# Attention heads on two groups of 64 TensorE rows, scores given from opposite groups, and a third PSUM bank for the row scores

## The chip, the cores and the metric

The kernel runs on one core of a Trainium2 chip. The metric is the device time of one execution in microseconds (us). TensorE is written PE (its weight loads PEld), VectorE DVE, ScalarE ACT, GpSimd POOL, and SyncE SP.

## What is computed

A macaron block on x of 16 items x 256 tokens x 128 features: half a mixture-of-experts layer (8 experts, the best 2 for each token), attention, and half the same mixture again.

```python
x = x + 0.5 * ffn(layernorm(x), ...)
x = x + attn(layernorm(x), ...)
x = x + 0.5 * ffn(layernorm(x), ...)

# attn: 16 heads of 4 features, of the left 64 features of x, softmax over the keys
q = (left @ Wq.T).reshape(N, S, H, Dh)      # N=16, S=256, H=16, Dh=4
k, v = ...                                   # likewise
att = softmax(einsum('nqhd,nkhd->nqkh', q, k) / scale, axis=2)
out = einsum('nqkh,nkhd->nqhd', att, v).reshape(N, S, 64) @ Wo.T + bo
```

## The kernel before

The first mixture, the attention and the second mixture follow each other. In the attention each engine runs the same loop by hand-written order: `run_steps` goes over steps s = 0 to 18, and each step has 16 units k (`UR` = 16). In step s the row scores of item s are made, the column scores, exponentials and most of the values of item s - 2, the last values and the output of item s - 3, and the projection of item s + 2.

Head operands. `qa` and `ka` hold, per item (four buffers in turn), q and k split into bf16 pieces: 24 rows (`KP`), and 2 more rows (`KM` = 26) that bring in the row maxima against rows of ones. They are `[128, 16 heads, 256]`, and only 26 of the 128 rows hold anything; a matmul runs over all 128. SP fills them through DRAM: `sp_pieces` writes the pieces, `sp_operands` reads them back with six DMAs, `sp_max` adds the maxima with two.

Scores. Unit k of a step has two matmuls of `pe_rows` (line 896, two heads of one half of the queries, 256 keys each) into one PSUM bank, from which DVE takes the maxima (`dve_max`, line 1179), and two of `pe_cols` (line 880, head k) into bank 3 or 4, from which ACT takes exponentials (`act_exp`, line 1000). `pe_rows` has banks 0 and 1 in turn (`SA`) and so waits for the maxima of two units earlier (`attn_max_done`); `pe_cols` waits for the exponential of two units earlier (`attn_exp_done`).

PE's order in a unit is: the two `pe_cols` matmuls, then whatever `AT` puts into this unit (transposes of the normed x, of the maxima, of the outputs; the output product `pe_out`, line 958; the projection `pe_project`, lines 931 and 933), then the two `pe_rows` matmuls, then the values (`pe_values`, line 908, fp32, sixteen records for four heads, each head on its own 32 columns of the array) in units 1, 5, 9 and 13. All of it is fp32 but the scores and the maxima.

Banks 5 (values), 6 and 7 (`MISC_A`, `MISC_B`) serve the rest; `misc_free` makes a user of bank 6 or 7 wait for the one before it. From step 5 the routing of the second mixture is made inside these steps, in two halves: a step with odd s has statistics, norm, transpose (unit 6) and logits (unit 11, lines 275 and 278), the one after it the choice, the positions and, for some groups, the lists. The routing uses bank 2 for all of that, and nobody else does. DVE's `dve_residual` (line 1210) adds the output product to x in unit 12, `dve_otok` (lines 1197 and 1201) divides the outputs in units 6 and 10.

## Time and profile before

| what | us |
|---|---|
| median of three runs (range) | 837.45 (835.38 to 838.81) |
| the profiled execution | 832.24 |
| its span on the core | 830.5 |
| PE busy, share of the span | 616.5 (74%) |
| DVE busy | 431.9 (52%) |
| ACT busy | 343.6 (41%) |
| POOL busy | 378.1 (46%) |
| first row scores (start) | 283.4 |
| first and last item's maxima closed | 300.8 and 602.6 |

The page gives busy time over the whole span; what a change in the attention is worth is read from the stretch between 283 and 640 us alone. PE's matmuls are pipelined and the ends shown are modelled: two matmuls of a group that start 0.11 us apart are each shown 0.27 us long, so PE's use is read from starts, and the moment at which a result can be used from the start of the engine that waits for it.

### The profile page before, as it was taken

The page shows a single profiled execution, that of the slowest core. Times are in us where ns is not written, and L with a number is a line of the kernel's source. Part 1 is how long each engine was busy: PE and PEld are TensorE (multiplying, and loading weights), DVE is VectorE, ACT ScalarE, POOL GpSimd, SP SyncE. Part 2 cuts the span into 40 slices and gives each one's busy share as a digit, 9 for nine tenths or more (in the row PEclk, how much of TensorE's full clock was granted, in tenths as well). Part 3 has the DMA queues.
Part 4 walks back from the last instruction along what each step waited for, and adds up shares of the span by engine and source line. Part 5 has one row for each costly group of instructions (what it writes and reads, how often), then busy time and mean ns, then how long its engine had stood idle before and what let it go on. Part 6 is the DMA issues. An engine that isn't in the chain of part 4 may idle for free. (4 is left out here: it accounts for less than half of the span.)

```text
span 830.5 us, 14400 instructions
## 1 busy us (share of the span) xinstructions
PE 616.5 (74%) x4460; PEld 449.2 (54%) x4460; DVE 431.9 (52%) x1607; ACT 343.6 (41%) x806; POOL 378.1 (46%) x421
## 2 busy tenths in 40 slices
PE   4318877999971288898888788888866778999850
PEld 3216766889960125555444555554533567887740
DVE  7633333232331387678777777757743343344425
ACT  2003333455530015665555555645554333454430
POOL 4775342000017886444666665432231465555452
PEclk9998798999995558999999999979998788999995
DMA  9453344655511121111212111101000435544428
GB/s 298 131 169 124 124 135 131 198 163 176 173 45 39 56 70 47 43 48 47 64 50 64 51 61 47 54 34 45 15 19 18 141 120 166 174 155 145 136 64 301
DMA packets 65026, 86.01 MB, mean 104 GB/s; under 512 B 11096, under 2 KB 46648, under 8 KB 64152
## 3 DMA queue, kind: packets, MB, share of 16 engines
q1 hardware_dynamic: 52184, 63.29, 23.6%
q0 software_dynamic: 8640, 17.97, 7.0%
q10 hardware_dynamic: 4128, 3.83, 1.4%
q8 instruction: 37, 0.61, 0.3%
q14 instruction: 37, 0.30, 0.1%
HBM read 31.85 MB, written 30.56 MB: 75 GB/s over the span
## 5 line engine op out<-in xcount | busy, mean ns | idle before, releaser
L1179 DVE TENSOR_REDUCE attn_nm<-ps 128x2 f32<-128x512 f32 x256 | 168.7, 685 | 71.7 <-PE ps L896 65.6
L671 DVE SCALAR_TENSOR_TENSOR experts_act<-ps,route_cols,experts_silu 128x256 f32<-128x256 f32 x170 | 80.0, 483 | 201.9 <-ACT experts_silu L635 137.9
L1000 ACT ACTIVATE attn_pt<-ps 128x512 f32<-128x512 f32 x256 | 145.6, 594 | 93.8 <-PE ps L880 76.4
L603 PE MATMUL ps<-experts_xT,experts_w 128*128 128x256 f32 x680 | 178.9, 409 | 0.1
L379 POOL DMA_INDIRECT x_rows<-route_xn,route_rows x128 | 124.8, 975 | 83.6 <-DVE route_rows L363 48.9
L896 PE MATMUL ps<-attn_ka,attn_qa 128*128 128x256 bf16 x512 | 107.9, 298 | 47.6 <-DVE attn_nm L1179 36.4
L603 PEld LDWEIGHTS ps<-experts_xT,experts_w 128*128 128x128 f32 x680 | 131.4, 204 | 17.6 <-issue 0.5
L614 PE MATMUL ps<-w_table,experts_act 128*128 x680 | 106.8, 295 | 28.9 <-ACT experts_y_tokens L652 14.0
L635 ACT ACTIVATE experts_silu<-ps,route_cols 128x256 f32<-128x256 f32 x170 | 78.4, 476 | 108.8 <-PE ps L603 83.8
L614 PEld LDWEIGHTS ps<-w_table,experts_act 128*128 128x128 f32 x680 | 93.9, 199 | 35.4 <-issue 33.8
L880 PE MATMUL ps<-attn_qa,attn_ka 128*128 128x256 bf16 x512 | 101.5, 282 | 13.2 <-ACT attn_pt L1000 8.2
L707 POOL DMA_INDIRECT y_tokens<-experts_y_tokens,experts_to x78 | 74.7, 957 | 68.2 <-ACT experts_y_tokens L652 50.6
L896 PEld LDWEIGHTS ps<-attn_ka,attn_qa 128*128 128x128 bf16 x512 | 39.6, 101 | 87.8 <-DVE attn_nm L1179 56.4
L908 PE MATMUL ps<-attn_pt,attn_va 128*32 128x256 f32 x1024 | 73.8, 409 | 1.0 <-ACT attn_pt L1000 1.0
L880 PEld LDWEIGHTS ps<-attn_qa,attn_ka 128*128 128x128 bf16 x512 | 41.2, 100 | 56.8 <-issue 34.1
L1077 POOL DMA_INDIRECT attn_yg<-y_rows,route_y_at x64 | 62.2, 973 | 15.8 <-issue 14.7
L1104 POOL MEMSET attn_va<- 128x1024 f32 x5 | 4.8, 963 | 115.0 <-DMA y_rows<-experts_y_tokens 115.0
L592 PE MATMUL ps<-ident,experts_x 128*128 128x128 f32 x170 | 34.6, 288 | 14.3 <-issue 7.8
L908 PEld LDWEIGHTS ps<-attn_pt,attn_va 128*32 128x32 f32 x1024 | 27.8, 113 | 27.5 <-issue 11.0
L1101 POOL TENSOR_TENSOR attn_kqp<-attn_rem,attn_kqp 128x256 bf16<-128x256 f32 x16 | 10.7, 667 | 68.7 <-ACT attn_kqp L1041 68.7
L641 ACT ACTIVATE experts_xT<-ps 128x256 f32<-128x256 f32 x85 | 32.6, 383 | 21.0 <-PE ps L592 13.1
L592 PEld LDWEIGHTS ps<-ident,experts_x 128*128 128x128 f32 x170 | 24.3, 150 | 26.9 <-issue 12.0
(165 smaller groups left out, 733.3 us busy)
## 6 DMA issues: line engine op xcount, KB each, us to landing
experts_w<-w_table SPq DMA_DIRECT2D x85, 256.0 KB
experts_x<-x_rows SPq DMA_DIRECT2D x85, 132.0 KB
y_rows<-experts_y_tokens SPq DMA_DIRECT2D x46, 128.0 KB, 1.7
x_rows<-no_rows SPq DMA_DIRECT2D x24, 132.0 KB
kq_pieces<-attn_kqp SPq DMA_DIRECT2D x16, 192.0 KB
x_rows<-route_xn,route_rows POOLq DMA_INDIRECT x128
second_y<-y_tokens SPq DMA_DIRECT2D x8, 256.0 KB, 6.9
second_y<-y_tokens ACTq DMA_DIRECT2D x8, 256.0 KB, 7.3
```

The source lines that it names most:

```text
L379: nc.gpsimd.indirect_dma_start(out=x_rows[REGION_OF[group_part(g)] % 2][:, :], out_offset=to, in_=xn[:, g % RX, t, :], in_offset=None).the ...
L603: mm = pe.matmul(ps[:, q % 2 * 2 + k, w * SLOTS:(w + 1) * SLOTS], m["w"][:, q % WR, at + k * P:at + (k + 1) * P], m["xT"][:, q % 2], start ...
L614: pe.matmul(o, m["act"][:, q % 2, k, i * P:(i + 1) * P], of_expert(w2_table, e, k * P, P), start=(k == 0), stop=False)
L635: nc.scalar.activation(m["silu"][:, q % 2, k], ps[:, q % 2 * 2 + k, 0:SLOTS], ACT.Silu, bias=route["col"](part, at, k)).then_inc(silu_done, 1)
L671: nc.vector.scalar_tensor_tensor(out=m["act"][:, q % 2, k], in0=ps[:, q % 2 * 2 + k, SLOTS:2 * SLOTS], scalar=route["col"](part, at, CH + ...
L707: nc.gpsimd.indirect_dma_start(out=y_tokens[:, :], out_offset=to, in_=m["y_tokens"][:, q % YR, i, :], in_offset=None).then_inc(y_sent[q % ...
L880: mm = pe.matmul(ps[:, SBK[h % 2], kc * S:(kc + 1) * S], ka[sl][:, h, kc * P:(kc + 1) * P], qa[sl][:, h, :], start=True, stop=True)
L896: mm = pe.matmul(ps[:, SA[k], j * S:(j + 1) * S], qa[sl][:, h, qc * P:(qc + 1) * P], ka[sl][:, h, :], start=True, stop=True)
L908: mm = pe.matmul(ps[32 * j:32 * j + 32, O, (g % 2) * S:(g % 2 + 1) * S], va[b % VR][:, kc, NJ * g + j, :], pt[:, g % 2, j, kc * S:(kc + 1) ...
L1000: nc.scalar.activation(pt[:, g % 2, j, :], ps[:, SBK[h % 2], :], ACT.Exp, scale=SCALE).then_inc(exp_done, 1)
L1077: nc.gpsimd.indirect_dma_start(out=yg[:, b % YG, t, r, :], out_offset=None, in_=y_rows[:, :], in_offset=route["y_offset"](2 * b + t, r)).t ...
L1179: nc.vector.tensor_reduce(nm[:, qc, 2 * pair:2 * pair + 2], ps[:, SA[k], :].rearrange("p (j t) -> p j t", t=S), AX.X, ALU.max, negate=True ...
```

## The change

- `qa` and `ka` become `[128, 8, 256]`: heads 0 to 7 lie on rows 0 to 63, heads 8 to 15 on rows 64 to 127, 26 rows used of each 64. The score matmuls name their group of 64 rows (`tile_position`).
- `pe_cols` and `pe_rows` are given one matmul at a time and in turn. Row scores begin with the heads of the upper group (`row_unit`), column scores with those of the lower, so that neighbours in PE's order lie on opposite groups.
- The row scores have three banks (0, 1, 2), and wait for the maxima of three units earlier. Bank 2 was the routing's; the routing's transposes and positions go to bank 6, logits and part sums (`cols`) to bank 7, and they wait there for the user before them, as others now wait for them.
- The other work of a unit comes after the unit's scores. `AT` changes: turned 6, xT 9, otok1 5, oTs 8, out 10, logits 12, positions 4, cols 14 of the second step; ACT's and DVE's units follow (residual 11).
- SP's six operand DMAs become twelve of half the size, its two for the maxima become four, the one of ones two. The zeroing of `qa` and `ka` is halved.

```diff
-    SA = (0, 1) * 8
+    SA = (0, 1, 2)
+    HH = NH // 2
...
-    AT = dict(xT=8, otok0=11, project=13, mT=2, otok1=6, oTs=10, out=12, values3=1, values0=5)
+    AT = dict(turned=6, xT=9, otok0=11, project=13, mT=2, otok1=5, oTs=8, out=10, logits=12, values3=1, values0=5,
+              positions=UR + 4, cols=UR + 14)
+    USES = {MISC_A: ("positions", "turned", "xT", "otok0", "project"), MISC_B: ("mT", "otok1", "oTs", "out", "logits", "cols")}
...
+    def half(t, r):
+        return t[r * P // 2:(r + 1) * P // 2]
+
+    def row_unit(k):
+        r = 1 - k // HH
+        pair, qc = divmod(k % HH, 2)
+        return r * HH // 2 + pair, qc
...
-    def pe_cols(pe, b, sl, h):
+    def pe_cols(pe, b, sl, h, kc):
...
+        r, at = divmod(h, HH)
+        mm = pe.matmul(ps[:, SBK[h % 2], kc * S:(kc + 1) * S], half(ka[sl], r)[:, at, kc * P:(kc + 1) * P],
+                       half(qa[sl], r)[:, at, :], start=True, stop=True, tile_position=(r * P // 2, 0))
+        if kc:
+            mm.then_inc(cols_ready, 1)
...
-        if not first(n, ago):
-            wait(pe, max_done, n - ago + 1)
-        for j in range(2):
...
+            if not first(n, len(SA)):
+                wait(pe, max_done, n - len(SA) + 1)
+        r, at = divmod(2 * pair + j, HH)
+        mm = pe.matmul(ps[:, SA[n % len(SA)], j * S:(j + 1) * S], half(qa[sl], r)[:, at, qc * P:(qc + 1) * P],
+                       half(ka[sl], r)[:, at, :], start=True, stop=True, tile_position=(r * P // 2, 0))
...
         for k in range(UR):
-            if valid(s - 2):
-                pe_cols(pe, s - 2, (sl - 2) % 4, k)
+            for i in range(2):
+                if valid(s - 2):
+                    pe_cols(pe, s - 2, (sl - 2) % 4, k, i)
+                if valid(s):
+                    pe_rows(pe, s, sl, k, i)
...
-            if valid(s):
-                pe_rows(pe, s, sl, k)
...
-            if u == 11:
+            if u == AT["logits"]:
+                misc_free(pe, s, MISC_B, "logits")
                 route["pe_logits"](pe, GROUPS + g)
...
+        for r in range(2):
+            heads = slice(r * HH * S, (r + 1) * HH * S)
...
+            for n in (3, 2, 1):
+                sp.dma_start(kv[at:at + n * DH, :], kq[0:n, 0]).then_inc(ops_in, 16)
...
         for i in range(KM - KP):
-            sp.dma_start(qa[sl][KP + i:KP + i + 1], mT[NH * i:NH * i + NH, :]).then_inc(m_in, 16)
+            for r in range(2):
+                at = NH * i + HH * r
+                sp.dma_start(half(qa[sl], r)[KP + i:KP + i + 1], mT[at:at + HH, :]).then_inc(m_in, 16)
...
-                qa.append(sb(f"qa{i}", [P, NH, S], BF16)[:])
-                ka.append(sb(f"ka{i}", [P, NH, S], BF16)[:])
+                qa.append(sb(f"qa{i}", [P, HH, S], BF16)[:])
+                ka.append(sb(f"ka{i}", [P, HH, S], BF16)[:])
```

**PE, the end of units 11 to 13 in a step with a routing's first half.** Before (L896 row scores, L880 column scores, L275 and L278 logits, L958 output product; a row's waits in brackets):

```order
L896 MATMUL ps<-attn_ka,attn_qa 128x256 [waits attn_max_done]
L896 MATMUL ps<-attn_ka,attn_qa 128x256
L275 MATMUL ps<-gate_b_sb,ident 128x32 [waits route_xT_done]
L278 MATMUL ps<-gate_w_sb,route_xT 128x8 x4
L880 MATMUL ps<-attn_qa,attn_ka 128x256 [waits attn_exp_done]
L880 MATMUL ps<-attn_qa,attn_ka 128x256
L958 MATMUL ps<-wo,attn_oTs 128x128 [waits attn_oTs_copied]
L958 MATMUL ps<-wo,attn_oTs 128x128
L896 MATMUL ps<-attn_ka,attn_qa 128x256 [waits attn_max_done]
L896 MATMUL ps<-attn_ka,attn_qa 128x256
L880 MATMUL ps<-attn_qa,attn_ka 128x256 [waits attn_exp_done]
L880 MATMUL ps<-attn_qa,attn_ka 128x256
```

After (L927 row scores, L911 column scores, L285 and L288 logits, L963 the projection):

```order
L911 MATMUL ps<-attn_qa,attn_ka 128x256 [waits attn_exp_done]
L927 MATMUL ps<-attn_ka,attn_qa 128x256 [waits attn_max_done]
L911 MATMUL ps<-attn_qa,attn_ka 128x256
L927 MATMUL ps<-attn_ka,attn_qa 128x256
L285 MATMUL ps<-gate_b_sb,ident 128x32 [waits route_xT_done,attn_x_updated]
L288 MATMUL ps<-gate_w_sb,route_xT 128x8 x4
L911 MATMUL ps<-attn_qa,attn_ka 128x256 [waits attn_exp_done]
L927 MATMUL ps<-attn_ka,attn_qa 128x256 [waits attn_max_done]
L911 MATMUL ps<-attn_qa,attn_ka 128x256
L927 MATMUL ps<-attn_ka,attn_qa 128x256
L963 MATMUL ps<-attn_xT,wqk 128x256 [waits attn_norm_done,attn_xT_done]
```

The scores now alternate one by one; the logits have moved behind the scores of unit 12 and wait for `attn_x_updated`, the end of DVE's residual; the output product, which stood between the scores of unit 12, has moved to unit 10.

**DVE, from unit 10 of such a step on.** Before (L1197 and L1201 divide the outputs, L1179 is a maximum, L1210 the residual):

```order
L1197 RECIPROCAL attn_rsum<-ps 128x16 [waits attn_norm_done,attn_otok_ready]
L1201 TENSOR_TENSOR attn_otok<-ps,attn_rsum 128x2x32 [waits attn_oTs_ready,attn_recip_done]
L1179 TENSOR_REDUCE attn_nm<-ps 128x2 [waits attn_rows_ready] x2
L1210 TENSOR_TENSOR x_tokens<-x_tokens,ps 128x256 [waits attn_bias_added,attn_y_ready]
L1179 TENSOR_REDUCE attn_nm<-ps 128x2 [waits attn_rows_ready]
```

After (L1234 and L1238, L1216, L1247):

```order
L1234 RECIPROCAL attn_rsum<-ps 128x16 [waits attn_norm_done,attn_otok_ready]
L1238 TENSOR_TENSOR attn_otok<-ps,attn_rsum 128x2x32 [waits attn_oTs_ready,attn_recip_done]
L1216 TENSOR_REDUCE attn_nm<-ps 128x2 [waits attn_rows_ready]
L1247 TENSOR_TENSOR x_tokens<-x_tokens,ps 128x256 [waits attn_bias_added,attn_y_ready]
L1216 TENSOR_REDUCE attn_nm<-ps 128x2 [waits attn_rows_ready] x2
```

The residual stands one maximum earlier than it did.

**SP, one step in the middle of the attention.** Before, all operand DMAs of a step and the two of the maxima:

```order
L1271 DMA attn_ka<-kq_pieces 12x1x4096
L1271 DMA attn_ka<-kq_pieces 8x1x4096
L1271 DMA attn_ka<-kq_pieces 4x4096
L1275 DMA attn_qa<-kq_pieces 12x1x4096
L1275 DMA attn_qa<-kq_pieces 8x1x4096
L1279 DMA attn_qa<-kq_pieces 6x4096
L1284 DMA attn_qa<-attn_mT 1x16x256 x2
```

After, the last DMA of the first group of heads, the six of the second, and the four of the maxima:

```order
L1318 DMA attn_qa<-kq_pieces 6x2048
L1311 DMA attn_ka<-kq_pieces 12x1x2048
L1311 DMA attn_ka<-kq_pieces 8x1x2048
L1311 DMA attn_ka<-kq_pieces 4x2048
L1315 DMA attn_qa<-kq_pieces 12x1x2048
L1315 DMA attn_qa<-kq_pieces 8x1x2048
L1318 DMA attn_qa<-kq_pieces 6x2048
L1325 DMA attn_qa<-attn_mT 1x8x256 x4
```

The maxima's DMAs stand behind twelve others now, where they stood behind six.

## Rows read from the trace of the kernel before

**Rows 1.** Page, costliest group: xcount | busy us, mean ns | idle before, releaser

```profile
L1179 DVE TENSOR_REDUCE attn_nm<-ps 128x2 f32<-128x512 f32 x256 | 168.7, 685 | 71.7 <-PE ps L896 65.6
```

**Rows 2.** Busy time by attention step: stretch, length, busy us of each engine, clock, DMA

```profile
300.80:316.30 15.50, 12.41 (x46) 4.69 (x46) 13.01 (x27) 2.43 (x6) 13.53 (x16) 0.50 0.20 59
...
412.70:434.70 22.00, 17.83 (x169) 10.85 (x167) 16.82 (x62) 11.67 (x27) 13.46 (x15) 1.00 0.18 54
434.70:454.30 19.60, 16.52 (x160) 9.44 (x159) 14.78 (x44) 11.36 (x25) 12.40 (x14) 1.00 0.20 60
...
476.10:496.60 20.50, 17.96 (x159) 10.29 (x157) 14.71 (x45) 11.31 (x25) 12.42 (x15) 0.92 0.19 58
...
537.40:564.80 27.40, 23.62 (x168) 14.69 (x166) 16.96 (x61) 12.10 (x27) 7.04 (x8) 0.75 0.10 34
...
sum 301.80, PE 256.15 PEld 151.02 DVE 224.40 ACT 164.15 POOL 152.14; mean PE 17.08 PEld 10.07 DVE 14.96 ACT 10.94 POOL 10.14
```

**Rows 3.** Waits from 300 to 600: who waited, on whom, total us, times, longest

```profile
PE ps L896 <- DVE attn_nm L1179: 32.6, 57, 1.7
```

**Rows 4.** Timeline 444 to 453: start, us, engine, line, operation, tiles [idle before]

```profile
445.25 1.07 PE L908 MATMUL ps<-attn_pt,attn_va 128*32 128x256 f32 x16
...
447.57 0.38 PE L896 MATMUL ps<-attn_ka,attn_qa 128*128 128x256 bf16 x2
...
447.79 0.38 PE L880 MATMUL ps<-attn_qa,attn_ka 128*128 128x256 bf16 x2
...
448.10 0.71 PE L958 MATMUL ps<-wo,attn_oTs 64*128 64x128 f32 x4
...
448.74 0.39 PE L896 MATMUL ps<-attn_ka,attn_qa 128*128 128x256 bf16 x2
...
450.46 0.69 DVE L1179 TENSOR_REDUCE attn_nm<-ps 128x2 f32<-128x512 f32 x1 [1.16 <-PE ps L896]
```

**Rows 5.** Timeline at 716, eight full-array fp32 matmuls of 256 columns

```profile
716.05 1.95 PE L603 MATMUL ps<-experts_xT,experts_w 128*128 128x256 f32 x8
```

**Rows 6.** Timeline 384 to 394, a step with a routing's first half

```profile
384.92 0.60 PE L943 MATMUL ps<-ident,attn_oT 128*128 128x128 f32 x4
...
385.72 1.04 PE L278 MATMUL ps<-gate_w_sb,route_xT 128*128 128x8 f32 x8
385.85 0.22 DVE L1201 TENSOR_TENSOR attn_otok<-ps,attn_rsum 128x64 f32<-128x64 f32 x1
...
388.60 0.41 DVE L1210 TENSOR_TENSOR x_tokens<-x_tokens,ps 128x256 f32<-128x256 f32 x1
```

**Rows 7.** Five-microsecond windows (PEclk 1.00 is 2.4 GHz, 0.50 is 1.2 GHz)

```profile
475.00:480.00 5.00, 3.29 (x37) 1.63 (x37) 4.54 (x16) 2.85 (x7) 2.60 (x3) 1.00 0.28 74
480.00:485.00 5.00, 4.45 (x31) 2.40 (x32) 3.46 (x14) 2.44 (x6) 3.61 (x5) 0.69 0.28 91
555.00:560.00 5.00, 5.00 (x20) 3.53 (x20) 1.02 (x2) 1.19 (x2) 0.00 (x0) 0.50 0.00 0
```

**Rows 8.** SP's queue in two steps, and the matmul that comes next

```profile
307.92 1.22 SPq L1284 DMA_DIRECT2D attn_qa<-attn_mT  x2
...
315.24 0.64 PE L880 MATMUL ps<-attn_qa,attn_ka 128*128 128x256 bf16 x2
...
436.84 1.93 SPq L1271 DMA_DIRECT2D attn_ka<-kq_pieces  x3
...
440.69 1.17 SPq L1284 DMA_DIRECT2D attn_qa<-attn_mT  x2
...
453.15 0.38 PE L880 MATMUL ps<-attn_qa,attn_ka 128*128 128x256 bf16 x2
```

**Rows 9.** Timeline, start of attention

```profile
283.03 1.80 POOL L1110 MEMSET attn_ka<- 128x2048 uint32 x1
...
283.44 1.03 PE L896 MATMUL ps<-attn_ka,attn_qa 128*128 128x256 bf16 x4 [7.34 <-DMA attn_qa<-kq_pieces]
...
286.61 2.07 DVE L1179 TENSOR_REDUCE attn_nm<-ps 128x2 f32<-128x512 f32 x3
```

More of the change, by code:

```diff
@@ L207, in bank, with through @@
         return BANK[g]
+    def through(name, g):
+        part = group_part(g)
+        if name == "positions" and ends_part(g):
+            return [(prod_done, g + 1), (list_step, listing(part) + 1)]
+        return [dict(turned=(xT_done, g + 1), logits=(index_done, g + 1), positions=(prod_done, g + 1),
+                     cols=(cols_done, part + 1))[name]]
     def closed_parts(part):
```

153 lines of the change are left out of this document (78 added, 75 removed).

## The prediction

> **What bounds the kernel now.** I read first where the attention spends DVE's time. The costliest group of the page is the maxima of the row scores, 256 of 685 ns, with 71.7 us of idle time before them, 65.6 of it ended by PE [rows 1]. The stretches by step are the second view [rows 2]; each reaches from the row that closes one item's maxima (line 1187) to the next such row. The fifteen from 300.8 to 602.6 us take 301.8 us, 20.1 each, and over them (last row) DVE is busy 224.4 of 301.8 us, so it stands idle 77.4, 5.2 a step. The 22.0 us step from 412.7 has a routing's first half and 16.8 us of DVE work, the 19.6 us step from 434.7 the second half and 14.8. No engine is full, then: PE and DVE hold each other up. The waits show both directions. Besides DVE's wait for PE, PE's row scores wait 32.6 us for the maxima, 57 times, the longest 1.7 us [rows 3]: with two banks PE can be only two units ahead.
>
> The timeline shows where which wait ends last [rows 4]. In the last third of a step PE never rests: a score pair takes 0.22 us (starts 447.57 and 447.79), then the output product, then scores again, and the maximum of unit 12 starts only at 450.46, 1.16 us of DVE's time lost. Its scores started at 448.74 and are shown over at 449.13, so the result reached DVE 1.3 us late. In the first third, where DVE has the routing's or the item's statistics to make, DVE is the busy one and PE waits (4.54 and 3.29 of 5 us from 475 to 480) [rows 7]. A gain in PE's score time therefore counts in about a third of a step, and a longer lead of PE over DVE counts at its beginning.
>
> **The change part by part.** Steps that have both kinds of scores are s = 2 to 15, fourteen; six of them (5, 7, ... 15) carry a routing's first half.
>
> *Scores from opposite groups.* A unit costs PE 4 matmuls, two pairs of 0.22 us, 0.44 [rows 4]. If neighbours run side by side it is 0.22, if not 0.44: the saving is 0 to 0.22. The trace of before has no two row groups, but it has four column groups: sixteen fp32 records of 256 columns take 1.07 us [rows 4], eight on the full array 1.95 [rows 5], so 0.067 against 0.24 each, 3.6 times as fast with four groups. I take 0.21 a unit, that nearest row. It counts in five units (10 to 14) of a step: 1.05 us, ends 0 and 1.1.
>
> *The third bank.* PE may be one maximum further ahead, 0.69 us [rows 1], when its long stretch begins; it also covers that much of a late result. I take 0.69 once a step, ends 0 and 1.4 (twice a step, since the values of unit 5 or 9 begin a smaller such stretch).
>
> Together 1.74 us in each of the eight steps without logits: 13.9. In steps 0 and 1, with row scores alone and no neighbours on the other group, only the bank: 1.4.
>
> *Logits behind the residual.* This is a new wait: PE's logits in unit 12 wait for `attn_x_updated`, and behind them in PE's queue stand the scores of unit 13, the projection and the values, for which DVE and ACT wait. From the start of the outputs' transposes to the end of DVE's division is 1.15 us (384.92 to 386.07), then DVE makes one maximum, 0.69, and the residual, 0.41: 2.25 us [rows 1, 6]. PE has in this time the transposes (shown 0.60) and the scores of unit 12 (0.22): it waits about 1.4 us, and then the logits' 1.04 us [rows 6] follow, before which nothing of unit 13 can be given. That eats the 1.74. I leave these six steps 0.5 us each for what they gain in unit 5 and 9: 3.0, ends -1 and 1.7 a step. The other new waits in banks 6 and 7 are for releases at least two units old, and I cost them at nothing; DVE's and ACT's work of those units is their cover.
>
> *More changes of the array's shape.* Leaving the scores for the output product costs 0.31 us from start to start where 0.22 is usual (447.79 to 448.10) [rows 4], so about 0.1 for a change. Before, a step changed at the values (four times there and back), at the output product and the projection: 12 changes. After, output and projection have the scores' shape, and the transposes of mT, otok1, xT, oTs and otok0 have not: 16, and 2 to 4 more with routing. In the last third it is 4 instead of 6, in the middle third 8 instead of 4, half of which I put on the path: 0.2 us x 14 = 2.8 lost. The Trainium skill (TensorEngine Tiling (Array Packing), Key Properties) says that changing the tiling mode, not just the tile, drains the TensorE; by a full drain, of the length that the last matmul of a pair is shown to have, the loss would be some 7 us rather than 2.8. The row at 448.10 shows 0.1, and I stay with it.
>
> *DMAs.* SP issues six operand DMAs in 3.85 us (436.84 to 440.69) and the maxima's two after them [rows 8]. Twelve take 7.7 if an issue of half the size costs the same. In a later step the maxima's DMAs then start at 444.5 instead of 440.7, and the columns that need them start at 453.15 [rows 8]: 8.6 us are left, less what the step gets shorter, and that hides them. In the first steps it is not: the maxima of item 0 are issued from 307.92 and their columns start at 315.24 [rows 8]; 3.85 us later, and four (2.4 us) instead of two, they are all issued at 314.2, and PE waits for whatever their landing takes over 1 us. No row has that landing alone; I take a wait of 2, ends 0 and 4. At the start the first scores come at 283.44, ended by the operands' DMAs; DVE's first maximum at 286.61, held by POOL, which zeroes ka in 1.80 us (and qa before it) [rows 9]. Halving both gives DVE 1.8 us, twice the issues takes 3.85 from PE: between -1.8 and +3.3, I take 1. Together 3.0 lost.
>
> *The clock.* In the steps from 412.7 and 434.7 the granted clock is 1.00, the 2.4 GHz level [rows 2]. At 475 to 480 PE is busy 3.29 of 5 us, and in the window after that it falls for a part (0.69 on the mean) [rows 7]. Shorter scores leave PE less busy in the first third, so I expect such falls in most steps. The price of a short one: the step from 476.1 (0.92) is 20.5 us, that from 434.7 (1.00) with the same work 19.6 [rows 2]: up to 0.9, 0.4 as a mean over some eight: 3.0 lost.
>
> Sum: 13.9 + 1.4 + 3.0 - 2.8 - 3.0 - 3.0 = 9.5 us gained. The second mixture begins when the attention ends and shifts with it. Against the profiled execution, 832.24, that is 822.7; the median of the runs shown is 837.45, 5.2 above it, and the same 9.5 us make **828.0**.
>
> **The rivals.** (1) *DVE becomes the only bound.* Concurrency, the bank and the cover of late results work everywhere, and DVE's idle time falls to what the first step shows, 15.50 - 13.01 = 2.5 us [rows 2]. 14 steps with 5.3 instead of 2.5: 39 us, less 3 for DMAs: 801. For it: PE's waits for DVE show that PE could run ahead. Against it: logits, clock. (2) *No concurrency*: weights and matmuls of the two groups go one after the other. Left are the bank, 0.69 x 8 + 1.4 = 6.9, half of the six steps' 3.0, and the losses by shape and DMA (5.8), no fall of the clock: about 835. (3) *The clock stays low*, slower: once the low-activity first third takes it down, the half clock lasts, as it does from 555 to 560 us at least (0.50 throughout, the 1.2 GHz level), in a step of 27.4 us instead of 22.0 [rows 2, 7]: 5.4 us a spell. Four such spells more are 21.6, against 12.5 gained (the sum without its 3.0 for short falls): 846. It decides from three spells on. (4) *The change doesn't do what it says because SP sets the pace*: the half-size DMAs are issued and landed too slowly, and the maxima's rows come after the columns want them in every step; then a step stays near 20 us, 837.
>
> **How the numbers follow.** Forecast 0.43, (1) 0.18, (2) 0.14, (3) 0.16, (4) 0.09. The range takes in the forecast's ends, the larger part of (1) and of (3): 803 to 845. What a measurement can tell from no change is 0.5%, 4.2 us. Faster: 0.40 + 0.18 + 0.05 = 0.63; slower: 0.15 + 0.03 of (4) and (2) = 0.18; the rest, 0.19, within.
>
> **What would show it.** Concurrency: four score matmuls of a unit within about 0.22 us of starts, and L911 and L927 starting nearly together; 0.44 says rival 2. The bank: PE's wait for the maxima well below 32.6 us and DVE's wait for PE below 65.6. Logits: a PE wait of 1 to 2 us before L285 in six steps, ended by DVE's L1247. DMAs: a PE wait for the maxima's DMA at the first column scores, and 12 issues in 7 to 8 us; more such waits in later steps say rival 4. Clock: several windows of the attention below 1.00 where they were 1.00. I am wrong in size if steps without logits are not 1 to 2 us shorter than 19.6, and in sign if the half clock lasts over 7 us at a time.

## The result, and the profile of the changed kernel

The changed kernel takes 852.0 us, the median of 5 runs (842.6 to 853.4), the kernel before beside it 835.8. The ratio is 1.0175, 95% interval 1.012 to 1.023: slower by 15 us (16 by the medians) where I had forecast 9.5 faster, and above the upper end of my range, 845. The profiled execution took 842.55 us (span 840.7), the shortest of the five; against the 832.24 (span 830.5) of the profiled execution of before its span is 10.2 us longer. The granted clock is 0.851 in the mean; before it was 0.893.

The page first. The idle time before the maxima fell, as forecast, from 71.7 to 56.2 us [rows 1], but that before ACT's exponentials is 104.4 us, 93.8 before, and the scores, half as many rows high, are no shorter on the mean (310 and 319 ns, before 282 and 298). Columns: xcount | busy us, mean ns | idle before, releaser.

```profile
L1216 DVE TENSOR_REDUCE attn_nm<-ps 128x2 f32<-128x512 f32 x256 | 165.9, 684 | 56.2 <-PE ps L927 43.4
L1037 ACT ACTIVATE attn_pt<-ps 128x512 f32<-128x512 f32 x256 | 145.8, 595 | 104.4 <-PE ps L911 93.7
...
L911 PE MATMUL ps<-attn_qa,attn_ka 64*128 64x256 bf16 x512 | 107.7, 310 | 40.1 <-ACT attn_pt L1037 30.8
...
L927 PE MATMUL ps<-attn_ka,attn_qa 64*128 64x256 bf16 x512 | 109.8, 319 | 18.3 <-DMA attn_qa<-kq_pieces 11.1
```

The stretches by step stand in the same form as in [rows 2], now from one closing of the maxima (line 1224) to the next.

```profile
300.10:314.40 14.30, 10.54 (x42) 4.91 (x42) 12.19 (x27) 2.47 (x6) 11.56 (x15) 0.50 0.22 66
...
348.70:365.20 16.50, 12.86 (x152) 6.44 (x152) 13.46 (x33) 11.43 (x26) 8.52 (x11) 1.00 0.20 56
...
388.80:411.00 22.20, 16.61 (x145) 7.14 (x137) 14.89 (x45) 10.69 (x22) 11.14 (x13) 0.73 0.16 47
411.00:434.30 23.30, 19.58 (x188) 9.14 (x187) 17.38 (x61) 13.27 (x29) 14.71 (x17) 0.83 0.19 56
434.30:453.00 18.70, 12.56 (x137) 6.37 (x136) 14.81 (x44) 10.22 (x23) 11.07 (x13) 1.00 0.19 57
...
536.50:563.40 26.90, 20.21 (x182) 11.02 (x186) 17.23 (x61) 13.13 (x29) 7.34 (x9) 0.79 0.13 40
...
sum 305.40, PE 238.93 PEld 115.24 DVE 226.72 ACT 164.89 POOL 149.68; mean PE 15.93 PEld 7.68 DVE 15.11 ACT 10.99 POOL 9.98
```

The fifteen steps take 305.4 us instead of 301.8 [rows 2], and DVE stands idle in 78.7 of them, as good as before (77.4): what the maxima gained was lost elsewhere. The steps split into three kinds. The four without routing (s = 1 to 4, of which the first and the last are shown) take 65.1 us, before 71.6: 6.5 gained. The six that give logits (s = 5, 7, ... 15; shown from 411.0 and 536.5) take 144.1, before 133.9: 10.2 lost. The five between them (shown from 388.8 and 434.3) take 96.2, before 96.3: nothing. The column of the granted clock (the third from the end) points at one reason: most steps are no longer at 1.00, and the step from 388.8 at 0.73 takes 22.2 us, that from 434.3 at 1.00 takes 18.7. It isn't the whole reason, since 411.0 and 536.5 are logits steps too. If f is the granted clock of a stretch of t us, 2(1 - f)t of it ran at the lower level, 1.2 GHz: 78 us of the eleven steps from 365.2 to 605.5, in 16 falls, and 21 before, in 4. Thirteen of the 16 spells are short, some 3 us; the longest two last 13.7 us. The end of the attention, in which only column scores are left, shows it once more. First the changed kernel, then the kernel before:

```profile
605.50:647.70 42.20, 34.07 (x257) 15.29 (x255) 13.65 (x80) 20.77 (x42) 8.96 (x9) 0.71 0.05 14
```

```profile
602.60:639.80 37.20, 26.82 (x261) 14.41 (x257) 13.98 (x81) 20.85 (x42) 8.95 (x9) 0.94 0.05 16
```

Sum of the span: -0.7 to the end of the first step, -6.5, +10.2, -0.1, +5.0 in this last stretch and +2.3 in the second mixture make 10.2.

The waits, 300.1 to 605.5 us: who waited, on whom, total us, times, longest.

```profile
ACT attn_pt L1037 <- PE ps L911: 83.6, 70, 5.2
...
DVE attn_nm L1216 <- PE ps L927: 42.9, 38, 2.9
...
PE ps L285 <- DVE x_tokens L1247: 7.1, 5, 1.9
...
PE ps L927 <- DVE attn_nm L1216: 4.2, 10, 0.9
...
PE ps L911 <- DMA attn_qa<-attn_mT: 2.0, 1, 2.0
```

PE's wait for the maxima is 4.2 us; it was 32.6 [rows 3]. The logits wait 7.1 us for the residual, 1.4 a time. Here is one, in a step with a routing's first half (start, us, engine, line, operation, tiles, idle before):

```profile
508.70 0.41 DVE L1247 TENSOR_TENSOR x_tokens<-x_tokens,ps 128x256 f32<-128x256 f32 x1
...
509.02 0.68 DVE L1216 TENSOR_REDUCE attn_nm<-ps 128x2 f32<-128x512 f32 x1
...
509.16 0.41 PE L285 MATMUL ps<-gate_b_sb,ident 128*128 128x32 f32 x2 [1.41 <-DVE x_tokens L1247]
...
509.41 1.04 PE L288 MATMUL ps<-gate_w_sb,route_xT 128*128 128x8 f32 x8
...
510.38 0.28 PE L911 MATMUL ps<-attn_qa,attn_ka 64*128 64x256 bf16 x1
...
512.09 0.60 ACT L1037 ACTIVATE attn_pt<-ps 128x512 f32<-128x512 f32 x1 [3.03 <-PE ps L911]
512.13 0.69 DVE L1216 TENSOR_REDUCE attn_nm<-ps 128x2 f32<-128x512 f32 x1 [2.42 <-PE ps L927]
```

PE stands from its last scores until the residual, 1.41 us, then gives the gate's bias and the logits, and only at 510.38 the scores of unit 13. DVE had one maximum in hand (509.02) and ACT nothing. The scores are shown over at 510.77, but both engines start on them only at 512.09 and 512.13: ACT has lost 3.03 us, DVE 2.42. So there is a late result on top of the wait. A purer case stands in the step that starts at 434.3:

```profile
449.17 0.27 PE L927 MATMUL ps<-attn_ka,attn_qa 64*128 64x256 bf16 x1
...
449.42 0.96 POOL L389 DMA_INDIRECT x_rows<-route_xn,route_rows  x1 [0.30 <-issue]
451.69 0.60 ACT L1037 ACTIVATE attn_pt<-ps 128x512 f32<-128x512 f32 x1 [2.47 <-remote]
451.73 1.29 DVE L1216 TENSOR_REDUCE attn_nm<-ps 128x2 f32<-128x512 f32 x2 [2.05 <-remote]
...
452.43 0.27 PE L911 MATMUL ps<-attn_qa,attn_ka 64*128 64x256 bf16 x1 [2.99 <-ACT attn_pt L1037]
```

The last score starts at 449.17 and is shown 0.27 us long; ACT and DVE start 2.5 us after its start, 2.3 after its shown end, having stood idle for 2.47 and 2.05, and PE, which needs the banks that they free, for 2.99. POOL issues indirect DMAs in that time. In the trace of before, in the same routing, a result came 1.3 us after the shown end [rows 4]. What follows on the clock, over the time in which PE had nothing (columns as in the stretches by step):

```profile
449.70:452.90 3.20, 0.47 (x4) 0.22 (x4) 1.18 (x2) 1.21 (x3) 0.90 (x2) 1.00 0.12 40
453.10:456.30 3.20, 3.17 (x26) 0.99 (x26) 2.98 (x14) 1.66 (x3) 2.60 (x4) 0.50 0.30 82
```

PE is busy 0.47 of 3.2 us, still at 1.00, and behind that the clock is 0.50, the level of 1.2 GHz, while PE is busy 3.17 of 3.2. All 16 falls of the eleven steps come behind a stretch with such gaps, most of them smaller: before the one at 408.6, for example, PE is busy 1.83 of 3.3 us.

```profile
405.20:408.50 3.30, 1.83 (x24) 1.43 (x26) 2.35 (x6) 2.23 (x5) 0.00 (x0) 1.00 0.06 20
```

### The profile page after: what moved, and what is told of

Same layout as the page of the kernel before. It is cut to its first block and busy times, and to the rows that moved or that the text cites. A ratio compares the mean times of both kernels' runs of the same rounds, so it can differ in the third digit from the quotient of the medians.

```text
span 840.7 us, 14542 instructions
## 1 busy us (share of the span) xinstructions
PE 602.3 (72%) x4460; PEld 413.0 (49%) x4460; DVE 431.5 (51%) x1607; ACT 344.2 (41%) x806; POOL 372.7 (44%) x421
## 5 line engine op out<-in xcount | busy, mean ns | idle before, releaser
L1216 DVE TENSOR_REDUCE attn_nm<-ps 128x2 f32<-128x512 f32 x256 | 165.9, 684 | 56.2 <-PE ps L927 43.4
L1037 ACT ACTIVATE attn_pt<-ps 128x512 f32<-128x512 f32 x256 | 145.8, 595 | 104.4 <-PE ps L911 93.7
L911 PE MATMUL ps<-attn_qa,attn_ka 64*128 64x256 bf16 x512 | 107.7, 310 | 40.1 <-ACT attn_pt L1037 30.8
L927 PE MATMUL ps<-attn_ka,attn_qa 64*128 64x256 bf16 x512 | 109.8, 319 | 18.3 <-DMA attn_qa<-kq_pieces 11.1
L911 PEld LDWEIGHTS ps<-attn_qa,attn_ka 64*128 64x128 bf16 x512 | 36.5, 99 | 111.0 <-issue 56.4
L940 PE MATMUL ps<-attn_pt,attn_va 128*32 128x256 f32 x1024 | 89.2, 478 | 0.7 <-ACT attn_pt L1037 0.7
L927 PEld LDWEIGHTS ps<-attn_ka,attn_qa 64*128 64x128 bf16 x512 | 36.9, 103 | 32.3 <-DVE attn_nm L1216 14.5
L940 PEld LDWEIGHTS ps<-attn_pt,attn_va 128*32 128x32 f32 x1024 | 31.0, 127 | 32.6 <-issue 21.6
L602 PE MATMUL ps<-ident,experts_x 128*128 128x128 f32 x170 | 34.4, 287 | 13.7 <-DMA experts_x<-x_rows 7.1
L651 ACT ACTIVATE experts_xT<-ps 128x256 f32<-128x256 f32 x85 | 32.6, 383 | 24.7 <-PE ps L602 14.7
L251 POOL TENSOR_TENSOR route_rstd<-route_vare,neg_half 128x4 f32<-128x4 f32 x16 | 16.7, 1046 | 48.7 <-DVE route_vare L246 48.1
```

The lines of the kernel that those rows point to most:

```text
L911: mm = pe.matmul(ps[:, SBK[h % 2], kc * S:(kc + 1) * S], half(ka[sl], r)[:, at, kc * P:(kc + 1) * P], half(qa[sl], r)[:, at, :], start=Tru ...
L927: mm = pe.matmul(ps[:, SA[n % len(SA)], j * S:(j + 1) * S], half(qa[sl], r)[:, at, qc * P:(qc + 1) * P], half(ka[sl], r)[:, at, :], start= ...
L940: mm = pe.matmul(ps[32 * j:32 * j + 32, O, (g % 2) * S:(g % 2 + 1) * S], va[b % VR][:, kc, NJ * g + j, :], pt[:, g % 2, j, kc * S:(kc + 1) ...
L1037: nc.scalar.activation(pt[:, g % 2, j, :], ps[:, SBK[h % 2], :], ACT.Exp, scale=SCALE).then_inc(exp_done, 1)
L1216: nc.vector.tensor_reduce(nm[:, qc, 2 * pair:2 * pair + 2], ps[:, SA[(UR * b + k) % len(SA)], :].rearrange("p (j t) -> p j t", t=S), AX.X, ...
```

## The experiments

The kernel before was timed again in each comparison, and it is not equally quick on every chip: 835.8 us beside the changed kernel above, 819.0, 739.5, 821.0, 820.2 and 831.5 in the five comparisons below. So every result is a ratio to the kernel before in its own comparison, with its 95% interval.

Three theories stood at the start. **A**: the shorter scores let PE's clock fall, and that eats more than the overlap of the two groups gives. **B**: the logits' wait and the shared banks. **C**: the doubled number of SP's DMAs.

### First comparison (the kernel before: 819.0 us)

**e1: the same 64 rows for both scores of a unit.**

```
-        r = 1 - k // HH
+        r = k // HH
```

> One line differs from the changed kernel: the row scores go through the heads in the other order, so that the row scores of a unit stand on the same 64 rows as its column scores and the four matmuls of a unit can only follow each other (0.44 us instead of 0.22). Nothing else moves. Theory A (the shorter scores leave PE so little to do that its clock falls, and the half clock costs more than the overlap gives): mean granted clock back from 0.85 to about 0.89, no more half-clock stretches than before the change, time 828 to 838, 15 to 20 us below the changed kernel's 852. Theory B (the logits' wait behind the residual and the shared banks 6 and 7): the waits stay, 850 to 858. Theory C (twelve and four DMAs on SP instead of six and two): also unchanged, 850 to 858.

Measured: 875.2 us, 1.059 (1.048 to 1.070), granted clock 0.79 to 0.81. All three theories are wrong about this one. Neighbours now can't overlap, and they don't:

```profile
350.78 0.28 PE L911 MATMUL ps<-attn_qa,attn_ka 64*128 64x256 bf16 x1
350.90 0.27 PE L927 MATMUL ps<-attn_ka,attn_qa 64*128 64x256 bf16 x1
```

A unit of four takes 0.44 us; in the changed kernel two start together, and the next two 0.12 us later, 0.23 a unit:

```profile
446.07 0.28 PE L911 MATMUL ps<-attn_qa,attn_ka 64*128 64x256 bf16 x1
446.07 0.28 PE L927 MATMUL ps<-attn_ka,attn_qa 64*128 64x256 bf16 x1
...
446.19 0.27 PE L911 MATMUL ps<-attn_qa,attn_ka 64*128 64x256 bf16 x1
...
446.30 0.27 PE L911 MATMUL ps<-attn_qa,attn_ka 64*128 64x256 bf16 x1
```

So the overlap is real and worth having, about 4% against 1.019 of the changed kernel in a comparison of like speed (below). But longer scores did not bring the clock back, as A had it: PE is busier (677 us instead of 602) and the clock lower. The low spells are fewer and much longer. One begins at 589.6, behind 3.2 us in which PE was busy 0.64, and lasts 44 us, with PE shown busy throughout:

```profile
589.60:633.80 44.20, 44.20 (x261) 23.27 (x262) 25.38 (x79) 19.02 (x36) 9.50 (x10) 0.50 0.09 28
```

**e2: one group of rows, the rest of the change kept** (operands, DMAs and score order of before; three banks; routing in banks 6 and 7).

```
-        r, at = divmod(h, HH)
-        mm = pe.matmul(ps[:, SBK[h % 2], kc * S:(kc + 1) * S], half(ka[sl], r)[:, at, kc * P:(kc + 1) * P],
-                       half(qa[sl], r)[:, at, :], start=True, stop=True, tile_position=(r * P // 2, 0))
+        mm = pe.matmul(ps[:, SBK[h % 2], kc * S:(kc + 1) * S], ka[sl][:, h, kc * P:(kc + 1) * P],
+                       qa[sl][:, h, :], start=True, stop=True)
...
```

> The changed kernel with its first part undone: the heads on one group of rows with six operand DMAs and the scores in the order of before (columns first, rows behind the unit's other work); three banks and the routing in banks 6 and 7 stay. A: no more clock falls, the third bank's gain is left, 825 to 835. B: the loss stays, 845 to 855. C: also 825 to 838, so that this run alone doesn't tell A from C.

Measured: 818.1 us, 0.994 (0.990 to 0.999). The expected 825 to 835 went with a kernel before of 835.8, and as a ratio 0.994 lies among them. The loss is gone, and the gain is small. The run takes away the two groups together with their DMAs and their order of scores; f2 and z1 below show that, with full rows, neither of these costs anything.

**e3: the two groups alone**, on the kernel before (two banks, routing in bank 2, all units as before).

```
-    SA = (0, 1) * 8
+    SA = (0, 1)
+    HH = NH // 2
...
+            for i in range(2):
+                if valid(s - 2):
+                    pe_cols(pe, s - 2, (sl - 2) % 4, k, i)
+                if valid(s):
+                    pe_rows(pe, s, sl, k, i)
...
```

> The kernel before with the first part of the change alone: two groups of rows, scores given in turn, twelve and four DMAs; two banks for the row scores, the routing in bank 2 and all other work in its units of before. A: clock falls as in the changed kernel, 845 to 860. B: the logits wait for nothing, and the overlap gains what I forecast, 820 to 830. C: as A, 845 to 855.

Measured: 851.3 us, 1.036 (1.027 to 1.044), clock 0.83. The groups lose 3.6% without any logits' wait and with two banks, so B is not the whole cause. A or C is left for this part.

**e4: every score matmul given twice.**

```
+        for _ in range(2):
             mm = pe.matmul(ps[:, SBK[h % 2], ...
...
```

> The changed kernel with every score matmul of the attention given twice in a row (the second writes the same result again), so that PE does twice the score work, as long as before the change, on both groups of rows. A: the clock rises to 0.90 or more and the time falls by 10 to 20 us although PE has more to do, 832 to 842. B and C: nothing to gain, 0.44 us more in each unit of the stretches where PE sets the pace, 855 to 870.

Measured: 870.9 us, 1.061 (1.056 to 1.067), clock 0.87 to 0.88. The clock does rise from 0.85, and it doesn't pay: PE's added work costs more. That is about the upper end of what B and C had given.

e1 and e4 suggested a new form of A: not how long PE is busy, but on how many of its rows. In e1 PE is busy longer than in the kernel before (677 us against 616.5), and the clock falls further.

### Second comparison (739.5 us)

**f1: the kernel before with its scores on 64 rows.** The other rows hold zeros, so that the result is the same.

```
-                           qa[sl][:, h, qc * P:(qc + 1) * P], ka[sl][:, h, :], start=True, stop=True)
+                           qa[sl][0:P // 2, h, qc * P:(qc + 1) * P], ka[sl][0:P // 2, h, :], start=True, stop=True)
...
```

> The kernel before with one difference: the score matmuls take the 64 rows of PE that hold the pieces, instead of all 128 of which the upper 70 are zeros. Nothing is given side by side, no DMA, order or bank differs, and the matmuls are as long. Theory A in its new form (PE's clock follows how much of the array works, and scores on 64 rows halve that): mean granted clock 0.80 to 0.83 instead of 0.90, time 850 to 865 where the kernel before has 819. Theory D (the loss of the two groups comes from side-by-side work itself or from the changes between the groups): no difference, 817 to 824. Theory C (DMAs): no difference either.

Measured: 843.0 us, 1.143 (1.137 to 1.149), clock 0.76 to 0.79 where the kernel before has 0.92. This is the largest effect of the study, more than twice what was expected, from an edit that moves and removes nothing. (Rows with something in them are 26 of 128, so 102 hold zeros, not 70.) Its step at 439.0, without logits:

```profile
439.00:460.10 21.10, 20.70 (x159) 10.60 (x158) 14.85 (x44) 11.72 (x25) 12.07 (x14) 0.76 0.18 56
```

and the same step of f2 (next), which has full rows and is as quick as the kernel before:

```profile
398.30:416.20 17.90, 15.97 (x158) 9.68 (x157) 14.73 (x44) 11.33 (x25) 12.30 (x14) 1.00 0.22 66
```

The matmuls are the same 158 or 159, DVE's work is 14.7 to 14.9 us in both, and the clock is 0.76 instead of 1.00. The 20.70 us of PE's busy time don't say that the clock fell under full work, since matmuls at the lower level take twice as long and so fill the step. What happened is seen when the stretch is cut where the level changes: before the fall at 415.1, then at the lower level, then behind the rise at 449.2.

```profile
411.60:415.00 3.40, 1.92 (x18) 1.00 (x22) 3.32 (x11) 1.98 (x5) 2.13 (x3) 1.00 0.23 61
415.20:449.20 34.00, 34.00 (x188) 17.91 (x180) 18.28 (x64) 13.40 (x27) 14.80 (x18) 0.50 0.15 47
449.30:460.10 10.80, 10.40 (x95) 6.08 (x94) 7.93 (x16) 6.95 (x16) 6.46 (x8) 1.00 0.09 27
```

The fall comes behind gaps, as in the changed kernel. But then PE is busy 34.00 of 34.00 us, on half of its rows, and the level stays at 1.2 GHz. This repeats every two steps, with the same 34 us. So what the halved rows take away is above all the return of the clock: f2 falls once in its fifteen steps, for a short spell, and the longest low spell that begins in these steps of the kernel before is 10 us. Falls without a gap exist too, two of f1's seven. Behind this stretch the clock is 0.50 again:

```profile
377.70:380.90 3.20, 3.20 (x27) 2.60 (x26) 1.77 (x4) 1.04 (x2) 0.00 (x0) 1.00 0.00 0
```

Both such stretches have the logits in them, eight matmuls of only 8 columns shown 1.04 us long, so that "busy" is not "full". More changes of shape between scores and transposes are no rival for f1's loss: at the full clock its pairs of scores start 0.22 us apart and lose 0.1 at a change, as before [rows 4]. The Trainium skill (TensorE: Matmul & The Clock Gate, HAM oscillation) ties falls of the clock to gaps in which PE has no matmuls. The late result at 449 of the changed kernel agrees with it, and so do five of f1's seven falls; two do not.

**f2: SP's DMAs cut as in the changed kernel**, twelve and four, on tiles of before.

```
+        for half in range(2):
+            heads = slice(half * HH * S, (half + 1) * HH * S)
...
```

> The kernel before with SP's DMAs cut as in the changed kernel: the operands in twelve instead of six, each with half of the heads, the maxima in four instead of two. Tiles, matmuls, order and banks are those of before. A: 819 to 823, only the first steps lose. C (twelve and four DMAs are what costs): 840 or more. My prediction's own term was 3.0 us.

Measured: 738.0 us, 0.998 (0.996 to 1.000). C falls; my term of 3.0 us for DMAs was a loss that isn't there.

**e6: the logits one unit later.**

```
-    AT = dict(turned=6, xT=9, otok0=11, project=13, mT=2, otok1=5, oTs=8, out=10, logits=12, values3=1, values0=5,
+    AT = dict(turned=6, xT=9, otok0=11, project=13, mT=2, otok1=5, oTs=8, out=10, logits=13, values3=1, values0=5,
...
-            if u == 14:
+            if u == 15:
                 route["dve_top"](dve, GROUPS + g)
```

> The changed kernel with the logits one unit later (13 instead of 12) and the top values behind unit 15 instead of 14. If PE's wait for the residual (7.1 us in five logits steps of the changed kernel's trace) is on the path, 845 or a little less, 5 to 7 below the changed kernel; if the clock sets the time of these steps, no difference, 850 to 854.

Measured: 726.5 us, 0.981 (0.978 to 0.984), clock 0.89 to 0.90. Faster than the kernel before, on a quick chip; whether by the edit or by the chip this comparison doesn't tell, and it was repeated below.

**f5: one matmul on all 128 rows more in each unit**, overwritten by the row scores.

```
+        if j == 0:
+            pe.matmul(ps[:, SA[n % len(SA)], 0:S], qa[sl][:, 0, 0:P], ka[sl][:, 0, :], start=True, stop=True)
```

> The changed kernel with one matmul more in each of the 256 units, on all 128 rows of PE, 256 columns, whose result the row scores overwrite: 0.11 us each, 28 us of PE's time in all, of which the stretches where PE sets the pace would pay about 10. A: the array works more, the mean granted clock rises from 0.84 to 0.87 or more, and the time is no longer than the changed kernel's, 840 to 852. If array work has nothing to do with the clock: clock 0.84, time 860 or more.

Measured: 784.3 us (775.3 to 790.3), 1.063 (1.055 to 1.071), profiled clock 0.90. The expectation had named times of the slower chip. Against e6 in the same comparison it is 58 us more, most of which the logits' unit can't be; the clock is no help at that price.

### Third comparison (821.0 us)

**g0: the changed kernel itself.**

> The changed kernel itself, on the chip on which the next three run, since the kernel before took 835.8, 819.0 and 739.5 us in three comparisons and the loss may depend on what makes the difference. Where the kernel before has 0.90 or less of mean granted clock, 1.01 to 1.02 of its time; where it is as quick as 740 us, 0.98 to 1.00, because the logits one unit later gave 0.981 there.

Measured: 836.8 us, 1.019 (1.011 to 1.027), clock 0.847. The result repeats on a second chip.

**g1: e6 again, beside it.**

> The changed kernel with the logits in unit 13 and the top values behind unit 15, again, now beside the changed kernel. If the wait for the residual is on the path: 5 to 7 us less than the changed kernel in the same comparison. If the clock sets the time of these steps: within 2 us of it.

Measured: 819.3 us, 0.998 (0.994 to 1.002). That is 17.5 us less than the changed kernel, 2.1%: the whole loss, and more than either side of the expectation had. Its six logits steps take 121.7 us in its trace, against 144.7 in that of g0, and the five between them give 6.5 of it back (103.7 and 97.2). One logits step of each, g0 first; the second has slightly more of the full clock and is 2.9 us shorter:

```profile
450.30:473.00 22.70, 18.97 (x187) 9.27 (x183) 17.17 (x61) 12.67 (x28) 14.45 (x16) 0.87 0.19 57
```

```profile
441.70:461.50 19.80, 16.46 (x168) 8.60 (x170) 15.68 (x46) 12.14 (x27) 13.66 (x16) 0.91 0.20 60
```

**g2: e2 again, one group of rows.**

> The third bank and the moved routing without the two groups of rows, again (the run of this edit before had 0.994 of the kernel before). Against the changed kernel in the same comparison this is the price of the two groups: 10 to 20 us below the changed kernel where the kernel before has a granted clock of 0.90 or less, and within 10 us of it or above it where it has 0.92.

Measured: 815.8 us, 0.994 (0.991 to 0.998), 21 us below the changed kernel. Two of its steps, and the sum of its fifteen:

```profile
428.70:447.00 18.30, 14.60 (x137) 8.89 (x137) 14.76 (x43) 10.32 (x23) 11.10 (x13) 1.00 0.19 57
447.00:469.30 22.30, 19.39 (x188) 11.83 (x188) 17.12 (x62) 13.12 (x29) 14.80 (x17) 1.00 0.19 58
...
sum 290.40, PE 249.26 PEld 149.61 DVE 224.95 ACT 165.46 POOL 153.19; mean PE 16.62 PEld 9.97 DVE 15.00 ACT 11.03 POOL 10.21
```

The clock is 1.00 in ten of its eleven steps with routing; in g0 in none. Its step without logits takes 18.3 us, the logits step, with the same wait for the residual, 22.3. Against g0 its six logits steps take 136.5 us instead of 144.7, the five between them 90.0 instead of 97.2. So of what the logits steps of the changed kernel lost against the kernel before (133.9), most goes with the two groups, and with one group they lose little.

**g3: g1 with the scores of units 0 to 5 given twice.**

```
+        for _ in range(2 if k < 6 else 1):
             mm = pe.matmul(ps[:, SA[n % len(SA)], ...
...
```

> The logits one unit later as in the run before last, and the scores of units 0 to 5 of each step given twice, where PE waits for DVE in any case: 24 matmuls more a step, some 1.3 us of PE's time if side by side. Clock theory: mean granted clock up by 0.02 to 0.04, time 5 to 15 us below the same kernel without the doubles. If PE's waits there are shorter than the doubles, or the falls come from the rest of the step: no gain, 0 to 15 us more.

Measured: 830.9 us, 1.010 (1.003 to 1.018), clock 0.875 (g1: 0.859). The clock rises by 0.016, and the time by 12 us. Filling PE with work to keep its clock has now failed in three forms.

### Fourth comparison (820.2 us)

**h1: one group of rows and later logits**, e2 and e6 together.

> One group of rows with the operands, DMAs and score order of before, three banks, the routing in banks 6 and 7, and the logits one unit later (13, top values behind unit 15). If the wait for the residual and the clock of the two groups are separate losses: the 17 us that the logits' move gave with two groups come off the 0.994 of one group, 0.972 to 0.98 of the kernel before. If the move only helps where the clock is low anyway: 0.99 to 0.994.

Measured: 807.3 us, 0.986 (0.983 to 0.990), profiled clock 0.903, between the two ends that were expected. It beats the kernel before by 1.4%, and the changed kernel by more than 3%. Two steps:

```profile
420.10:439.50 19.40, 15.92 (x157) 9.66 (x156) 15.88 (x59) 11.26 (x26) 12.30 (x15) 1.00 0.20 61
439.50:459.20 19.70, 17.72 (x167) 11.25 (x168) 15.67 (x46) 11.99 (x27) 13.60 (x16) 1.00 0.19 60
```

The logits steps are down from 22.3 (g2) to 19.7, those between up from 18.3 to 19.4: the later logits push work into the next step.

**h2: h1 with two banks for the row scores.**

```
-    SA = (0, 1, 2)
+    SA = (0, 1)
```

> The kernel of the run before this with two banks for the row scores instead of three, all else the same. My term for the third bank was 0.69 us in each of fourteen steps, 9.7 in all, and so 8 to 11 us more than that kernel; up to 20 if late results make the bank worth more; within 2 us of it if the bank is worth nothing.

Measured: 814.4 us, 0.993 (0.989 to 0.996). The third bank gives 0.6%, 5 us by the ratios and 7 by the medians, less than the 8 to 11. The two intervals just touch.

**h3 and h4: the changed kernel with two banks**, h4 with the logits in bank 7 as in the changed kernel, h3 with them in the free bank 2, in the same unit, where no residual stands in their way.

```
-    LOGITS = BANK[:GROUPS] + (7,) * GROUPS
+    LOGITS = BANK[:GROUPS] + (2,) * (GROUPS - 1) + (7,)
...
-                misc_free(pe, s, MISC_B, "logits")
```

> The changed kernel with two banks for the row scores, and the logits of the six steps in the free bank 2, still in unit 12, where they wait for nothing but their own operands. Against the next run (the same with the logits in bank 7, waiting for the residual): if the wait is what the later unit removed, 10 to 18 us less; if the later unit helped by its place, within 3 us.

> The changed kernel with two banks for the row scores instead of three, all else the same. Third bank worth its 0.69 us a step: 1.03 of the kernel before where the changed kernel has 1.019; bank worth nothing with two groups, because the clock takes it back: 1.015 to 1.02.

Measured: h3 860.4 us, 1.053 (1.047 to 1.059); h4 877.4 us, 1.068 (1.063 to 1.073). With two banks the wait for the residual costs 17 us by the medians and 12 by the ratios. But with two banks it is also longer than in the changed kernel, where it was 7.1 us (4.5 in g0): over the fifteen steps of h4 (301.1 to 647.8) the trace has

```profile
PE ps L285 <- DVE x_tokens L1247: 14.1, 6, 4.0
```

so that this pair doesn't show that a wait costs much more than its own length, and it doesn't say how much of g1's 17.5 us was the wait. With two groups the third bank is worth 1.068 against 1.019 (g0), some 40 us, where up to 1.03 had been expected for two banks: eight times what it is worth with one group.

### Fifth comparison (831.5 us)

**z1: h1 with the changed kernel's order of scores** (in turn, ahead of the unit's other work), still on all rows; **z2: h1 again.**

```
+            for i in range(2):
+                if valid(s - 2):
+                    pe_cols(pe, s - 2, (sl - 2) % 4, k, i)
+                if valid(s):
+                    pe_rows(pe, s, sl, k, i)
```

> One group of rows, three banks, later logits, and the scores in the changed kernel's order, a column and a row score in turn ahead of the unit's other work. If the price of the two groups (0.998 against 0.986 of the kernel before) is the 64 rows' and the clock's: within 3 us of the next run. If it is the order's: 5 to 10 us more than the next run, near 0.998 of the kernel before.

> One group of rows, three banks, later logits, the scores in the order of before, again beside the run ahead of it: 0.983 to 0.990 of the kernel before.

Measured: z1 814.1 us, 0.980 (0.975 to 0.985); z2 817.3 us, 0.986 (0.979 to 0.993). The order costs nothing; if anything it helps, and z1 is, by its ratio, the best kernel on the chips of like speed, though the two intervals overlap. z1 and g1 (0.998) differ in the groups of rows alone, with their DMAs and the order of the heads: 1.8%. PE has gaps in z1 as well, and the clock stays at 1.00 over most of them. Here is one, with the 12 us behind it:

```profile
444.80:448.10 3.30, 1.62 (x13) 0.98 (x12) 1.52 (x4) 1.56 (x4) 1.28 (x2) 1.00 0.13 41
448.20:460.00 11.80, 10.17 (x104) 5.93 (x102) 10.53 (x37) 7.68 (x17) 9.16 (x11) 1.00 0.26 77
```

In the fifteen steps the clock falls 17 times in the changed kernel and in g0, 14 times in g1, twice in h1 and z1, once in g2, and six times in the kernel before.

## Why the prediction was wrong

Put together, as ratios to the kernel before on chips of like speed: the moved routing and third bank give 0.994 (g2); the two groups on top of it 1.019 (g0). With later logits the two are 0.986 (h1) and 0.998 (g1). So two things ate the gain: the groups of 64 rows, 1.2 to 2.4% with three banks (3.6% with two, e3), and the unit of the logits, 0.8% with one group and 2.1% with two. Each makes the other dearer. By the terms of the prediction:

**Scores from opposite groups: right in itself.** Four scores take 0.23 us instead of 0.44, and without the overlap the same kernel is 4% slower (e1). The term counted only this.

**The clock: the step that failed.** I had 3.0 us for short falls, eight times 0.4, and took the reason to be PE's shorter busy time alone. That halving the rows changes how the clock behaves I put at nothing. In f1 it costs 14% with no score shorter or side by side: on the quick chip the clock falls behind gaps and then stays low for 34 us in which PE is never shown idle. In the changed kernel, where both groups work at once, most spells are short again, but there are 16 in the eleven steps with routing where there were 4, and they have 78 us at the lower level, before 21. With the overlap's gain already in it, the groups' price is 10 us (g1 against h1, 0.998 - 0.986 of 820), 15 (g1 against z1) or 20 (g0 against g2), against the 3.0. In e1, without the overlap, PE is busy longer and the kernel slower still, so shorter scores can't be the whole reason; how many of the changed kernel's falls are due to the rows and how many to PE's longer gaps no run separates. My rival 3, the half clock, was the nearest: slower, 846, for which I had 0.16, and my range ended at 845, below it. But its mechanism, four long spells more, isn't what came: only two of the 16 last over 7 us.

**The third bank: 9.7 us forecast in fourteen steps, 5 to 7 measured** with one group (h2), some 40 with two (h4 against g0). Why it is worth so much more there isn't settled. In the changed order a row score that waits for its bank also holds the unit's column scores behind it, which speaks for stretches in which PE, DVE and ACT all stand and the clock falls, and h4 has 139 us at the lower level in its eleven steps with routing, g0 79. The wait for the maxima by itself isn't it: without the third bank it rises by some 20 us in both cases (from 3.9 to 25.7 us from h1 to h2, from 6.2 to 27.4 from g0 to h4). No run separates the rest.

**Logits behind the residual: the wait was forecast well, its price wrong.** 1.4 us forecast, 7.1 / 5 = 1.4 seen. But I let the six steps gain 0.5 us each, and they lost 1.7 each. Most of that is the two groups' (g2, with one group and the same wait, has 136.5 us in them, 0.4 lost each). The rest I had left out: DVE has one maximum in hand and ACT nothing when PE comes back, and the first result after that is late too, so that 2.42 and 3.03 us of idle time stand where I had counted on the gain of the other units to cover the wait. Moving the logits one unit later gave 17.5 us with two groups, nearly 3 a step. How much of that is the wait and how much the new place stays open. My ends, -1 and 1.7 a step, were too narrow.

**Steps without routing: right.** The four are 6.5 us shorter (65.1 for 71.6), forecast 0.7 for the first and 1.74 for each of the others, 5.9. That the sum fits so well is in part luck: one by one they gain 1.2, 0.7, 1.6 and 3.0, and the last is at 1.00 where it was at 0.91 before. The five steps between logits should have gained 1.74 each and gained nothing: that from 434.3, at clock 1.00, took 18.7 us for 19.6 [rows 2], but that from 388.8, at 0.73, took 22.2.

**Changes of shape: the price of one is right, the sum of 2.8 us untested.** From the pair of row scores at 445.17 to the transposes behind it there is 0.31 us in the changed kernel's trace, as from the scores to the output product before [rows 4]. A full drain at each change, as the Trainium skill has it (TensorEngine Tiling (Array Packing), Key Properties), to the length that the last matmul of a pair is shown to have (0.38), would have shown more.

**DMAs: 3.0 us forecast, nothing measured** (f2). The issues take what I said, twelve in 7.55 us:

```profile
435.11 1.90 SPq L1311 DMA_DIRECT2D attn_ka<-kq_pieces  x3
...
442.66 1.34 SPq L1325 DMA_DIRECT2D attn_qa<-attn_mT  x2
```

At the start, the scores come 3.4 us later [rows 9], DVE's first maximum 0.9:

```profile
286.86 3.19 PE L927 MATMUL ps<-attn_ka,attn_qa 64*128 64x256 bf16 x12 [8.69 <-DMA attn_qa<-kq_pieces]
...
287.50 1.89 DVE L1216 TENSOR_REDUCE attn_nm<-ps 128x2 f32<-128x512 f32 x3 [0.43 <-PE ps L927]
```

and the first column scores wait 2.0 us for the maxima's DMAs, the very value taken. But they start at 314.9 us, no later than the 315.24 of [rows 8], because the steps ahead of them are shorter by as much: the cover was there, and I had counted the wait without it.

What stays open: why results of PE reach ACT and DVE up to 2.3 us late. In the traces read it happens while POOL issues its indirect DMAs, but no run here takes these away, since the routing needs them. It was there before the change. Also open is what makes one chip take 739.5 us for what takes 820 to 836 on others; there DVE's idle time before the maxima is 47.1 us (f2) instead of 71.7 [rows 1], and the changed kernel with later logits gained 1.9% instead of 0.2.

## What to carry to other kernels

Halving the rows that a matmul uses can cost more than running two side by side gives: look at the granted clock of the stretches after such a change, and price it by a kernel that differs in the rows alone. Where the clock is low, cut the stretch where the level changes and look at what the engine did before; the busy share of a slow stretch is high because it is slow. A wait that PE takes in the middle of its queue is best priced by what the engines behind it have in hand when it ends; one unit of room for the logits was worth 17 us here with two groups and 7 with one. And take a change of several parts apart at once: on chips of like speed the best kernels of this study have all of it but the two groups, with the logits one unit later.

## What the runs showed of the hardware

With its scores on 64 rows, one at a time, PE stood at the lower level for 34 us while shown busy for all of them (f1), and for 44 us in e1; with scores on 128 rows the longest low spell that began in the same steps was 10 us (before, g2). With two groups of 64 rows side by side most low spells were short, but the clock fell 14 to 17 times in fifteen steps, against one or two times in the like kernels with full rows (g2, h1, z1) and six in the kernel before. Adding work to PE raised the clock (0.847 to 0.876 with all scores given twice, 0.859 to 0.875 with six units' scores), and never the speed. Two matmuls on opposite groups of 64 rows start within 0.01 us of each other, and four take 0.23 us at 2.4 GHz. A result of PE can reach the other engines 2.3 us after the matmul is shown to be over. And the same kernel took 739.5 us on one chip and 819 to 836 on others.
